# A graph network's attention sums: half of the count multiplies on POOL, with a relu pass on ACT in place of their cap

## What is computed

```python
e = leaky_relu(a_src[src] + a_dst[dst], 0.2)
m = segment_max(e, dst)
ex = exp(e - m[dst])
alpha = ex / segment_sum(ex, dst)[dst]
out = segment_sum(alpha * h[src], dst) + bias
```

## Time and profile before

| what | value |
|---|---|
| time, median of 3 runs | 6705.4 us (6697.15 to 6705.66) |
| span of the profiled execution | 7945.8 us |
| own time of the profiled execution | not given apart from its span |
| PE busy | 4874.7 us (61%) |
| DVE busy | 4588.3 us (58%) |
| ACT busy | 1702.0 us (21%) |
| POOL busy | 2560.5 us (32%) |
| first call of gat_sums, its units | from about 4183 to 4890 us of the span |
| second call, its units | from about 5311 to 6020 us |

### The profile page before, as it was taken

How to read it: one execution, slowest core, us unless ns; L and a number is a source line. 1 busy time by engine, 2 the same in 40 slices (tenths; PEclk the granted TensorE clock), 3 DMA queues, 4 the chain that set the end, 5 groups by cost and what they waited for, 6 DMA issues and landing times. The chain is left out here.

```text
span 7945.8 us, 66561 instructions
## 1 busy us (share of the span) xinstructions
PE 4874.7 (61%) x19050; PEld 3113.7 (39%) x19050; DVE 4588.3 (58%) x7164; ACT 1702.0 (21%) x3179; POOL 2560.5 (32%) x2457
## 2 busy tenths in 40 slices
PE   2511011776247777787998888878886986233333
PEld 1200001665225555555883333853333443232323
DVE  7501111999846667687889998989994002011112
ACT  0100000444012222200444554014552003000000
POOL 0677776000035657672000000000000000666664
PEclk9999999999978888898559999569998998555556
DMA  2000000000423333311553333743333665111111
GB/s 67 3 2 2 2 2 3 8 8 22 122 88 111 105 105 121 112 48 32 154 149 105 110 113 97 196 124 109 114 114 148 264 241 142 47 46 46 46 46 42
DMA packets 429673, 679.01 MB, mean 85 GB/s; under 512 B 88837, under 2 KB 310691, under 8 KB 419611
## 3 DMA queue, kind: packets, MB, share of 16 engines
q1 hardware_dynamic: 350770, 565.26, 21.8%
q0 software_dynamic: 78576, 109.51, 5.1%
HBM read 533.71 MB, written 140.88 MB: 85 GB/s over the span
## 5 line engine op out<-in xcount | busy, mean ns | idle before, releaser
L1086 POOL DMA_INDIRECT ring<-rel_dram,rel_pair x806 | 765.7, 950 | 3498.4 <-SPq L71 3113.3
L996 PE MATMUL total<-to,from 128*128 128x256 f32 x2816 | 855.0, 438 | 374.3 <-issue 300.7
L1117 PE MATMUL total<-ring,onehot 128*128 128x128 f32 x1612 | 448.7, 423 | 713.6 <-issue 646.9
L817 POOL DMA_INDIRECT cells_dram<-rec,place x752 | 795.5, 1058 | 267.4 <-issue 234.4
L879 POOL DMA_INDIRECT ring<-l_dram,src_pair x600 | 669.0, 1115 | 512.4 <-POOLq L71 201.6
L1652 PE MATMUL sums<-acc,hw 128*64 128x392 f32 x2144 | 745.5, 504 | 137.3 <-DVE acc L1586 136.9
L518 PE MATMUL node<-moved,onehot 128*128 128x75 f32 x1568 | 372.2, 413 | 713.0 <-issue 562.0
L996 PEld LDWEIGHTS total<-to,from 128*128 128x128 f32 x2816 | 529.7, 210 | 648.6 <-issue 596.7
L1097 DVE TENSOR_SCALAR onehot<-iota,loc_pair 128x128 f32<-128x128 f32 x806 | 176.5, 302 | 986.9 <-remote 792.4
L1117 PEld LDWEIGHTS total<-ring,onehot 128*128 128x128 f32 x1612 | 341.1, 289 | 821.8 <-issue 820.6
L518 PEld LDWEIGHTS node<-moved,onehot 128*128 128x128 f32 x1568 | 351.5, 326 | 740.8 <-issue 574.3
(11 more groups left out here) (390 smaller groups left out, 8552.8 us busy)
## 6 DMA issues: line engine op xcount, KB each, us to landing
count<-ac_dram SPq DMA_DIRECT2D x200, 784.0 KB, 4.1
strip<-ac_dram SPq DMA_DIRECT2D x75, 1600.0 KB, 6.5
ac_dram<-stage SPq DMA_DIRECT2D x125, 640.0 KB
h<-ac_dram SPq DMA_DIRECT2D x26, 1600.0 KB, 9.6
acc<-ac_dram SPq DMA_DIRECT2D x24, 1600.0 KB, 9.6
lo_row<-lo_dram SPq DMA_DIRECT2D x102, 256.0 KB
rel_dram<-rows SPq DMA_DIRECT2D x25, 1024.0 KB, 5.4
mask_dram<-mask SPq DMA_DIRECT2D x25, 800.0 KB
```

The costliest lines, as they stand in the source:

```text
L817: pool.indirect_dma_start(m.cells_dram[:, :], bass.IndirectOffsetOnAxis(ap=m.place[:, j:j + 1], axis=0), m.rec[:, j, :], None, bounds_chec ...
L996: nc.tensor.matmul(spots[:, at(spot), :].rearrange("p o n -> p (o n)"), from_[:, n % 2, u, :], to[:, n % 2, u, :, :].rearrange("p k d -> p ...
L1086: pool.indirect_dma_start(ring[:, j % SLOTS, :], None, m.rel_dram[:, :], bass.IndirectOffsetOnAxis(ap=m.rel_pair[:, j:j + 1], axis=0)).the ...
L1117: last = nc.tensor.matmul(total[:, at(col, D)], onehot[:, j % U, :], ring[:, j % SLOTS, :], start=False, stop=False, skip_group_check=True)
```

## The change

In every odd unit the weigh moves from DVE to POOL. POOL has no operation here that takes the min and multiplies in one, so the odd units are kept finite in another way: ACT first computes `relu(-(z + bias))`, which is the exponent held at zero or below and negated (with `less` = minus the bias), waits for itself, and then takes `exp(-that)`. Even units stay as they were. The wait on `weighed` becomes a wait on one of two semaphores by the parity of the unit (`unit_weighed`), on SP, DVE and PE. `Z` is a name for the 4 that was there, and changes nothing. `less` is made once in a call, by a DVE instruction of 100 elements a partition.

```diff
+        less, lowered = sb("less", [P, NT, HEADS]), sem("lowered")
+        def unit_weighed(eng, n):
+
+            eng.wait_ge(weighed_pool if n % 2 else weighed, n // 2 + 1)
+
+        @block.gpsimd
+        def _(pool):
+            for n in range(1, last_unit, 2):
+                pool.wait_ge(count_in[n // 2 % 2], 16 * (n // 4 + 1))
+                pool.wait_ge(exped, n + 1)
+                if n >= 3:
+                    pool.wait_ge(used, n - 2)
+                nc.gpsimd.tensor_tensor(p[n % 3], z[n % Z], count[:, n // 2 % 2, :], ALU.mult).then_inc(weighed_pool, 1)
...
@@ sync
-                    sp.wait_ge(weighed, 2 * (n - 1))
+                    unit_weighed(sp, 2 * n - 4)
+                    unit_weighed(sp, 2 * n - 3)
...
@@ scalar
-                nc.scalar.activation(z[n % 4], z[n % 4], ACT.Exp, bias=a_src[:, 1, t, k:k + 1]).then_inc(exped, 1)
+                if kk:
+                    nc.scalar.activation(z[n % Z], z[n % Z], ACT.Relu, scale=-1.0, bias=less[:, t, k:k + 1]).then_inc(lowered, 1)
+                    act.wait_ge(lowered, n // 2 + 1)
+                    nc.scalar.activation(z[n % Z], z[n % Z], ACT.Exp, scale=-1.0).then_inc(exped, 1)
+                else:
+                    nc.scalar.activation(z[n % Z], z[n % Z], ACT.Exp, bias=a_src[:, 1, t, k:k + 1]).then_inc(exped, 1)
...
@@ vector, peak
-                if n >= 4:
-                    dve.wait_ge(weighed, n - 3)
+                if n >= Z:
+                    unit_weighed(dve, n - Z)
...
@@ vector
+            v.tensor_scalar(less[:, :, :], a_src[:, 1, :, :], -1.0, None, ALU.mult)
...
                 if kk == 0:
                     dve.wait_ge(count_in[n // 2 % 2], 16 * (n // 4 + 1))
-                dve.wait_ge(exped, n + 1)
-                if n >= 3:
-                    dve.wait_ge(used, n - 2)
-                v.scalar_tensor_tensor(p[n % 3], z[n % 4], FLOOR, count[:, n // 2 % 2, :], ALU.min, ALU.mult).then_inc(weighed, 1)
+                    dve.wait_ge(exped, n + 1)
+                    if n >= 3:
+                        dve.wait_ge(used, n - 2)
+                    v.scalar_tensor_tensor(p[n % 3], z[n % Z], FLOOR, count[:, n // 2 % 2, :], ALU.min, ALU.mult).then_inc(weighed, 1)
...
@@ tensor
-                pe.wait_ge(weighed, n + 1)
+                unit_weighed(pe, n)
```

More of the change, by code:

```diff
@@ L1410 @@
 UNITS = 2 * NT
+Z = 4
 BLOCKS = -(-HALF // P)
@@ L1432, in gat_sums @@
         psum = ps("sums", [P, 8, 512])
-        peaked, exped, weighed, used = (sem(n) for n in ("peaked", "exped", "weighed", "used"))
+        peaked, exped, weighed, weighed_pool, used = (sem(n) for n in ("peaked", "exped", "weighed", "weighed_pool", "used"))
+        less, lowered = sb("less", [P, NT, HEADS]), sem("lowered")
         diag_made, lifted, laid = (sem(n) for n in ("diag_made", "lifted", "laid"))
@@ L1544, in peak @@
                     dve.wait_ge(laid, 16 * i + 8 * (kk + 1))
-                if n >= 4:
-                    dve.wait_ge(weighed, n - 3)
-                v.scalar_tensor_tensor(z[n % 4], steep[:, i % 2, kk, :], a_src[:, 0, t, k:k + 1], flat[:, i % 2, kk, :], ALU.add, ALU.max).then_inc(peaked, 1)
+                if n >= Z:
+                    unit_weighed(dve, n - Z)
+                v.scalar_tensor_tensor(z[n % Z], steep[:, i % 2, kk, :], a_src[:, 0, t, k:k + 1], flat[:, i % 2, kk, :], ALU.add, ALU.max).then_inc(peaked, 1)
             def divide(i):
@@ L1571, in _ @@
             v.memset(minus[:, :], -1.0)
+            v.tensor_scalar(less[:, :, :], a_src[:, 1, :, :], -1.0, None, ALU.mult)
             turn(0, 0)
             turn(0, 1)
-            peak(0)
-            peak(1)
+            for n in range(Z // 2):
+                peak(n)
             for n in range(last_unit):
@@ L1578, in _ @@
                 u = n % UNITS
-                if n + 2 < last_unit:
-                    peak(n + 2)
+                if n + Z // 2 < last_unit:
+                    peak(n + Z // 2)
                 if kk == 0:
                     dve.wait_ge(count_in[n // 2 % 2], 16 * (n // 4 + 1))
-                dve.wait_ge(exped, n + 1)
-                if n >= 3:
-                    dve.wait_ge(used, n - 2)
-                v.scalar_tensor_tensor(p[n % 3], z[n % 4], FLOOR, count[:, n // 2 % 2, :], ALU.min, ALU.mult).then_inc(weighed, 1)
+                    dve.wait_ge(exped, n + 1)
+                    if n >= 3:
+                        dve.wait_ge(used, n - 2)
+                    v.scalar_tensor_tensor(p[n % 3], z[n % Z], FLOOR, count[:, n // 2 % 2, :], ALU.min, ALU.mult).then_inc(weighed, 1)
                 if i:
```

## The result

The changed kernel takes 7014.54 us (median of 4 runs, 7003.99 to 7016.94) against 6702.48 us: a ratio of 1.0462, 95% interval 1.045 to 1.0475, or 312 us more. Its profiled execution spans 7015.1 us.

The account below looks back on a forecast made before the run. DVE was taken as the bound at 6.93 us a pair; with DVE and POOL taking turns, 5.31 + 0.08 + 3.5 = 8.89 us, +1.96 x 200 = +392 us on 6705.4, giving 7097 us, range 6930 to 7290.

Parts of the forecast that it names:

- The bound, and the weigh that goes: In the changed stage DVE is the bound; losing one 1.70 us weigh leaves it 5.22 us a pair of units.
- The relu on ACT, costed at nothing: The added ACT pass makes ACT's pair 4.66 us, which fits under DVE's 5.22, so it adds no time.
- The multiply, 3.5 us: POOL's two-input multiply of 1568 elements in odd units, taken between 2.88 and 4.32 us.
- The exclusion, read off three indirect DMAs: Three sparse-stage cases suggest POOL's SBUF reads wait for DVE instructions with two SBUF inputs, so little POOL work hides.
- The sum, 8.89 us a pair: DVE and POOL take turns: 5.31 on DVE, 0.08 of hand-overs, 3.5 multiply; against 6.93 before, +392 us.
- peak(n + 4): The DVE peak four units after POOL's unit n, forecast to stall for that multiply and so let POOL read.
- The single case at 3414.73: A sparse-stage indirect DMA took 1.97 us, 1.02 more, not let in between L924 and L919, which followed without a gap.
- the low end of the range at 0.2: DVE might use some 0.2 us of each multiply when POOL does not read, 40 us less in all.
- The signs named for it: Profile after: DVE idle about 3.6 us a pair before odd peaks, busy near 60% of the stage, pairs every 8.9 us.
- The count tiles on SP and the code loading on POOL: Late count loads stall DVE about 0.6 us at the weigh, sum unchanged; POOL's first-use code loading at most 15 us.
- The rival without exclusion: POOL's multiply runs beside DVE, leaving DVE's 5.22 us a pair as the bound: faster, 6378 us; chance 0.11.
- The rival with a cheap multiply: Exclusion holds but the POOL multiply takes 1.44 us: a pair of 6.83 us, 6685 us, about the same; chance 0.03.

Follow-up runs that it names:

- the run with the relu pass alone: The kernel before, with the relu pass of the odd units added on ACT, every weigh staying on DVE: 6695.6 us, ratio 1.0003.
- The memset: The kernel before, plus a POOL instruction in every odd unit that only writes zeros over 1568 columns, nobody waiting for it: 6695.2 us, ratio 1.0003.
- The copy: The kernel before, plus a POOL copy of one 1568-column tensor in every odd unit, nobody waiting for it: 6954.4 us, ratio 1.0384.
- the quarters run: The changed kernel with each peak and weigh of DVE issued in four pieces of 392 columns: 7211.4 us, ratio 1.0754 to the kernel before.
- the run without the relu: The changed kernel without the relu pass, odd units going from one exp straight to POOL's multiply: 7003.1 us, ratio 1.0458 to the kernel before.
- the late run: The changed kernel with a 400-column memset on POOL ahead of each multiply, some 0.4 us: 7016.1 us, ratio 1.0475 to the kernel before.
- the side multiply: The kernel before, plus a same-size POOL multiply of unrelated tensors in every odd unit, nobody waiting for it: 7353.2 us, ratio 1.0984.

## Why the prediction was right

The time, 7014.5 us, lies within 6930 to 7290, and slower had 0.86. The cause that was forecast, the exclusion of POOL's reads and DVE's two-input instructions, is the one that the runs show; the course of a pair was not as forecast, and the loss was put too high, at 392 us instead of 312. The extra length of the profiled execution before (7945.8 us) does not bear on it: its stage, at 1830.0 us, is as long as in the run with the relu pass alone (3081.8 to 4913.6, 1831.8 us), which spans 6693.2 in all. By its steps:

- **The bound, and the weigh that goes.** DVE's 5.22 us for two peaks and a weigh is what the profile after shows, apart from the 3.26 for which the one peak is held.
- **The relu on ACT, costed at nothing.** The relu-only run says so: 1.0003. ACT takes 1.60 and 1.51 us for the two passes, as the row of the exp gave it.
- **The multiply, 3.5 us.** Measured 3.52, and 3.49 at its shortest. The memset as a measure of one stream was sound too: 1.40 us for 1568 columns, where I had 1.44. The way from there to 3.5 was not, and that it came out is luck. I took a value between "writes beside reads" (2.88) and "one after the other" (4.32), because only some of the writing would fall beside reading. The copy, which reads and writes, takes 1.49 us, 0.09 more than the memset: nearly all of the writing falls beside the reading. An estimate by that, with two reads for one, is 2 x 1.49 = 2.98 us for the multiply, and why it takes 3.49 no run here shows. The price of the Trainium skill ("GPSIMD Engine Reference", "Elementwise — side-by-side cycle accounting"), an estimate of 3.44 us, was near too.
- **The exclusion, read off three indirect DMAs.** It holds. The rows had shown only POOL waiting; the runs show DVE waiting for POOL as well, and that one SBUF input on DVE or no reads on POOL end it. The Trainium skill ("SBUF — State Buffer", "Who interferes with whom") has these conditions: two SBUF inputs on DVE's side, a read of SBUF on POOL's, and not a POOL instruction that only writes. The runs agree, with 3.26 us for a multiply, 1.28 for a copy and nothing for a memset. That the second to issue waits for the first is borne out for the long instructions; in the quarters run a piece that DVE began 0.19 us after POOL's start (3260.21 against 3260.02) still ran before POOL's reads.
- **The sum, 8.89 us a pair, was 0.41 too long,** and this is the step that failed: that POOL "does not get its reads until DVE stalls", and DVE stalls "at peak(n + 4), which waits for just that multiply". DVE never waited for a semaphore there. POOL was let in at a change from one DVE instruction to the next, right after its exp, and what waited was peak(n + 2), whose buffer was long free, with its start already on record. The single case at 3414.73, in which POOL was passed over at such a change, had been taken for the rule. So the two hand-overs (0.08) and the lost overlap of DVE's last instruction (5.31 against 5.22, 0.09) do not occur, and DVE is held for 3.26 us, not for the full 3.5 (0.24). The three make 0.41, x 200 = 82 us, and 392 - 82 = 310. Without the first two, and with POOL's time without reads, which I had put only into the low end of the range at 0.2, the sum would have given 8.52. The signs named for it failed as well: DVE has no idle time before the odd peaks and is busy for all of the stretch, not for 60%. Read by its letter, the check "if DVE has no idle time and POOL's multiplies lie beside the peaks at full speed" would even have spoken against the exclusion, since DVE has none and POOL's 3.52 us does lie beside a peak; only the 5.10 us of that peak show that it stood still.
- **The count tiles on SP and the code loading on POOL.** Neither shows. Peaks and weighs have no idle time before them but the 41.5 us at the starts of the calls; POOL releases a count tile earlier than forecast, since it multiplies beside peak(n + 2) and not beside peak(n + 4). And the first multiply follows some 0.2 us behind the first exp of an odd unit (3096.8 + 1.5), against 0.13 for the later one above:

```profile
L1529 ACT ACTIVATE h<-h x100: 1509/1510/1516, 3096.8 to 5230.4; 128x1568 f32<-128x1568 f32 x100
```

```profile
3098.51 4.38 POOL L1472 TENSOR_TENSOR acc<-h,count 128x1568 f32<-128x1568 f32 x1 [501.68 <-ACT h L1529]
```

The first multiply is recorded as 4.38 us, 0.86 longer than 3.52, but it too waited for a DVE instruction to end: 3.36 back from its end at 3102.89 is 3099.53, and a peak ran from 3097.67 to 3099.51.

The rival without exclusion (6378 us) fell with the side multiply. The rival with a cheap multiply fell with its 3.52 us.

## What to carry to other kernels

Moving work from DVE to POOL relieves DVE only if the two can read at the same time. Where DVE's instructions have two SBUF inputs, a POOL instruction that reads SBUF costs DVE nearly its own length (3.26 of 3.49 us), so it pays only if it is shorter than what it takes off DVE; here 3.26 us were paid for 1.70. Beside DVE instructions with one SBUF input (the accumulating kind, and the TENSOR_TENSOR with its other input in PSUM; no other kind was tried), or with a POOL instruction that only writes, it cost next to nothing (0.03 us for a multiply, nothing measurable for a memset). A DVE that is busy without a gap is no proof that it works: compare the length of one instruction with its length before.

## What the runs showed of the hardware that I had not expected

DVE's wait for the reads stands in the profile as a longer instruction (5.10 us for 1.84), not as idle time, and POOL's as well (5.06 for 3.5). Which of the two gets the reads at a change of instruction is not settled. With DVE instructions of 1.7 to 1.9 us, POOL was let in at the end of the one that was running when it started (the changed kernel, the run without the relu, the late run). With short ones it sometimes had to let one more pass: the indirect DMA that waited behind L924 and L919, and the quarters. That an indirect DMA reads twice would explain the former but not the latter; neither was tried. And a DVE instruction with one SBUF input that also writes its accumulator follows the next at the same 1.70 us as the two-input weigh, with the reading of the accumulator hidden.
